# An RWKV block with a ternary feed-forward half: five tiles of lag, six-bank rounds and another order in the first tile

## The reference, cut to what matters

```python
xn = layernorm(x)                                   # eps 1e-5
# attention half (RWKV v4), input xn
h  = LN(xn) ; h1 = shift(h)                         # eps 1e-3, shift by one position
k, v, r = mix_k(h,h1) @ tm_Wk, mix_v(h,h1) @ tm_Wv, mix_r(h,h1) @ tm_Wr   # 1024x1024 each
wkv = running exponential-decay average of v weighted by exp(k)           # along the sequence
y  = xn + sigmoid(r) * wkv @ Wo
h  = LN(y) ; h1 = shift(h)
a  = y + sigmoid(mix(h,h1) @ cm_Wr) * (square(relu(mix(h,h1) @ cm_Wk)) @ cm_Wv)  # 1024->4096->1024
# feed-forward half, input xn as well
tern(W) = clip(round(W / mean|W|), -1, 1)           # over the whole 4096x1024 matrix
f  = gelu(xn @ tern(W1).T + b1) @ tern(W2).T + b2   # 1024->4096->1024
out = x + a + f
```

## Time and profile before

| what | us |
|---|---|
| median of 3 runs | 5135.28 |
| lowest of the runs | 5126.62 |
| profiled execution, device time | 5128.33 |
| its span on the slowest core (core 0) | 5126.5 |
| the other cores' spans | 5105.4 to 5123.9 |
| PE busy | 4776.4 (93%) |
| DVE busy | 2595.4 (51%) |
| ACT busy | 2131.2 (42%) |

### The profile page before, as it was taken

One profiled execution on the slowest core, in us unless ns is written; L12 is line 12 of the kernel. 1 busy time (PEld: TensorE's weight loads), 2 busy tenths in 40 slices (PEclk: granted clock), 3 DMA queues, 4 the chain that ended last, 5 costly groups with the idle time before them and its releaser, 6 DMA issues.

```text
span 5126.5 us, 63290 instructions; the slowest of 8 cores (5105.4 to 5126.5 us)
## 1 busy us (share of the span) xinstructions
PE 4776.4 (93%) x21484; PEld 2154.9 (42%) x21922; DVE 2595.4 (51%) x3424; ACT 2131.2 (42%) x3436; POOL 429.7 (8%) x807
## 2 busy tenths in 40 slices
PE   3577888799999999999999999999999999999999
PEld 1233333344444444444444444444444444444444
DVE  6746566666555545555554555545555554330111
ACT  2433756554544434354443435444343544342111
POOL 0000111122000000100000010000001000000111
PEclk8789999899999999999999999999999999999999
DMA  6477878899455564645556464555646455555765
GB/s 159 103 193 180 261 230 244 249 291 318 165 189 199 177 225 160 231 158 192 202 179 216 163 230 163 192 190 196 202 166 226 159 185 192 175 185 189 230 227 179
DMA packets 273339, 1021.40 MB, mean 199 GB/s; under 512 B 34432, under 2 KB 34560, under 8 KB 267008
## 3 DMA queue, kind: packets, MB, share of 16 engines
q1 hardware_dynamic: 194112, 706.83, 40.6%
q0 software_dynamic: 78768, 310.43, 20.7%
q10 hardware_dynamic: 144, 0.07, 0.0%
HBM read 916.52 MB, written 127.93 MB: 204 GB/s over the span
## 4 chain that ended last, share of the span: by engine, by line
PE 84%; DMA 7%; DVE 4%; issue 2%; ACT 2%; POOL 0%; another core or an unknown queue 0%; DVEq 0%; SPq 0%; ACTq 0%; POOLq 0%
PE pb L333 82%; DMA rb<-w2t 2%; DMA rb<-w1t 1%; DMA ra<-zwkvr 1%; PE pb L382 1%; PE pb L775 1%; DMA rb<-cwk 1%; DMA zw2t<-XC 1%; PE pb L779 1%; DVE xr L419 1%; DVE TT L414 0%; DMA x<-xS 0%; DVE xk L419 0%; DMA rb<-cwv 0%; ACT TT L376 0%
## 5 line engine op out<-in xcount | busy, mean ns | idle before, releaser
L333 PE MATMUL pb<-xk,rb 128*128 128x512 bf16 x8028 | 1785.6, 381 | 81.5 <-DVE xr L419 60.0
L333 PE MATMUL pb<-big,rb 128*128 128x512 bf16 x8034 | 1792.3, 379 | 16.9 <-DMA rb<-cwv 5.7
L333 PEld LDWEIGHTS pb<-xk,rb 128*128 128x128 bf16 x8192 | 802.7, 98 | 1051.9 <-issue 96.5
L333 PEld LDWEIGHTS pb<-big,rb 128*128 128x128 bf16 x8192 | 801.9, 98 | 979.2 <-issue 16.4
L796 ACT ACTIVATE RC<-pb 128x512 f32<-128x512 f32 x512 | 301.4, 589 | 725.5 <-PE pb L333 640.3
L703 ACT ACTIVATE big<-pb,vecs_s 128x512 bf16<-128x512 f32 x512 | 346.3, 686 | 563.9 <-PE pb L333 550.3
L735 DVE SCALAR_TENSOR_TENSOR RO<-pb,vecs_s,RO 128x512 f32<-128x512 f32 x128 | 95.9, 749 | 580.3 <-PE pb L333 386.2
L333 PE MATMUL pb<-xk,ra 128*128 128x512 bf16 x1005 | 255.6, 396 | 109.9 <-DMA ra<-zwkvr 44.8
L525 DVE TENSOR_TENSOR_SCAN W<-wdec,carry,pb 128x512 f32<-128x512 f32 x128 | 163.7, 1279 | 361.4 <-PE pb L333 361.4
L798 ACT ACTIVATE big<-RC 128x512 bf16<-128x512 f32 x512 | 322.5, 630 | 47.5 <-ACT RC L796 0.8
L838 DVE TENSOR_TENSOR RO<-pb,RC 128x512 f32<-128x512 f32 x113 | 77.9, 690 | 478.1 <-PE pb L333 478.1
(11 more groups left out here) (102 smaller groups left out, 3875.6 us busy)
## 6 DMA issues: line engine op xcount, KB each, us to landing
rb<-zw1t SPq DMA_DIRECT2D x256, 512.0 KB, 3.7
rb<-zw2t SPq DMA_DIRECT2D x256, 512.0 KB, 5.0
rb<-zcwk SPq DMA_DIRECT2D x240, 512.0 KB, 4.9
rb<-zcwv SPq DMA_DIRECT2D x240, 512.0 KB, 6.0
ra<-zwkvr SPq DMA_DIRECT2D x120, 768.0 KB, 7.2
resS<-RO POOLq DMA_DIRECT2D x128, 256.0 KB, 5.7
rb<-w1t POOLq DMA_DIRECT2D x64, 512.0 KB, 8.9
rb<-w2t POOLq DMA_DIRECT2D x64, 512.0 KB, 10.1
```

The source lines that it names most:

```text
L333: tok = PE(lambda t, k=k: t.matmul(pb[bank][:], slot[:, col + k * 128:col + (k + 1) * 128], rhs[k], start=start and k == 0, stop=stop and ...
```

## The change

Six things are changed together.

- `LAG` is 5: one more tile runs without a feed-forward half, and one more feed-forward half stands alone at the end. The ternary passes take a step each 5.2 us and then each 6.2 us of planned time in place of 4.2 and 5.2.
- `rounds` is new: it runs several blocks in several banks side by side, part of the reduction first. In the `LAG` tiles, six of the eight Wo blocks run over `att` pieces 0 to 6 in banks 2 to 7 as soon as piece 6 is there, and then over piece 7; six key blocks (`cwk_first`) run over each pair of `xk2` pieces as the mix delivers it. Three weight rows are released together at the end of such a round. The mixer of the next tile is held from the fourth Wo block on.
- In those tiles the k/v/r groups stand closer: first, every = (16, 4) for t = 0, (12, 4) for the middle ones, (12, 6) for the last, where they were (16, 5), (11, 5), (11, 7).
- The k/v/r rows 0 and 1 of tile 1 are fetched right after tile 0's groups; row g + 2 is fetched after group g, in place of row g + 1 before it.
- Weight loads of the start wait until all of the first `x` has landed; `R01` is made before `R0`, and `ln0_norm` waits for `R0` by its own name.
- `ln0_stats(1)` no longer stands before `wo_stage(0)`: it is chained in front of `ln0_mix(1)`, behind `ln2_apply(0)`.

The diff, cut at unchanged lines:

```diff
@@ -1,3 +1,4 @@
+import itertools
 import numpy as np
@@ -25,12 +26,12 @@
...
-LAG = 4
+LAG = 5
 NB_RING = 7
...
 BLOCK_NS = 1740.0
-SUM_NS = 4200.0
-WRITE_NS = 5200.0
+SUM_NS = 5200.0
+WRITE_NS = 6200.0
 LATE = 5
@@ -284,7 +285,7 @@
...
         rows = slice(row * 128, (row + 1) * 128)
-        ready = dma("gpsimd", f"G{ring.name}{i}", slot[:], wdram[w][rows, :], *ring.free[i])
+        ready = dma("gpsimd", f"G{ring.name}{i}", slot[:], wdram[w][rows, :], *ring.free[i], *x_in[0])
         back = dma("sync", f"W{ring.name}{i}", zdram[w][rows, :], slot[:], ready)
@@ -334,6 +335,21 @@
...
         return tok
+    def rounds(jobs, parts):
+        done = {}
+        for at, (ks, ready) in enumerate(parts):
+            for bank, slot, col, rhs, loaded in jobs:
+                for k in ks:
+                    w = [ready] if k == ks[0] else []
+                    if at == 0 and k == ks[0]:
+                        w += [loaded, *bank_free[bank]]
+                    tok = PE(lambda t, bank=bank, slot=slot, col=col, rhs=rhs, k=k: t.matmul(
+                        pb[bank][:], slot[:, col + k * 128:col + (k + 1) * 128], rhs[k], start=k == 0, stop=k == 7),
+                        w, inc=k == 7)
+                done[bank] = tok
+        return done
@@ -383,13 +399,12 @@
...
         tk["sq_free"] = t6
-        a1 = ACT(lambda s_: s_.activation(out=R0[:], in_=pb[bk2][:], func=AF.Ln, scale=1.0 / E, bias=LN0_EPS),
-                 t6, tk.get("ln0_done"), tk.get("norm_done"))
-        a2 = ACT(lambda s_: s_.activation(out=R01[:], in_=pb[bk2][:], func=AF.Ln, scale=(1.0 + LN_EPS) / E,
-                                          bias=LN0_EPS * LN_EPS))
-        bank_free[bk2] = [a2]
-        ACT(lambda s_: s_.activation(out=R0[:], in_=R0[:], func=AF.Exp, scale=-0.5), a1)
-        tk[f"rstd{j}"] = ACT(lambda s_: s_.activation(out=R01[:], in_=R01[:], func=AF.Exp, scale=-0.5), a2)
+        for r, key, scale, eps in ((R01, "rstd", (1.0 + LN_EPS) / E, LN0_EPS * LN_EPS), (R0, "rstd0", 1.0 / E, LN0_EPS)):
+            a1 = ACT(lambda s_, r=r, scale=scale, eps=eps: s_.activation(
+                out=r[:], in_=pb[bk2][:], func=AF.Ln, scale=scale, bias=eps),
+                t6, tk.get("ln0_done"), tk.get("norm_done"))
+            tk[f"{key}{j}"] = ACT(lambda s_, r=r: s_.activation(out=r[:], in_=r[:], func=AF.Exp, scale=-0.5), a1)
+        bank_free[bk2] = [a1]
@@ -460,9 +475,11 @@
...
         cur = xn[j % 2]
+        while f"rstd0{j}" not in tk:
+            yield -2000.0
         for p in range(4):
             tn = DVE(lambda v, p=p: v.tensor_mul(pair(cur, p), pair(x, p), twice(R0)),
-                     tk[f"rstd{j}"], tk.get(f"x2_free{j % 2}"))
+                     tk[f"rstd0{j}"], tk.get(f"x2_free{j % 2}"))
             yield 1220.0
@@ -505,6 +522,7 @@
...
                     yield cost
+                tk[f"mix2_{pend[3]}"] = tk["mixed"]
             elif p == 0:
@@ -564,7 +582,7 @@
...
         def last():
-            wk["nd_free"] = tk["att"] = DVE(lambda v: v.tensor_mul(ck(att, g), ND[:, 0, :], ND[:, 1, :]), l2,
+            wk["nd_free"] = tk[f"att{g}"] = DVE(lambda v: v.tensor_mul(ck(att, g), ND[:, 0, :], ND[:, 1, :]), l2,
                                             tk.get("wo_done"))
@@ -577,8 +595,6 @@
...
         unit = fetch("wkvr", g)
-        if t == 1 and g + 1 < EC:
-            prefetch("wkvr", g + 1)
         toks = []
@@ -588,6 +604,8 @@
...
         release(unit, toks[-1])
+        if t == 1 and g + 2 < EC:
+            prefetch("wkvr", g + 2)
         tk["kvr_done"] = toks[-1]
@@ -743,16 +761,25 @@
...
-    def wo_stage(t):
+    def wo_stage(t, split=False):
         short["banks"], short["at"] = [2, 3, 4, 5, 6, 7], 0
         cur = xn[t % 2]
-        unit = None
-        ev = None
+        rhs = [ck(att, k) for k in range(8)]
+        units, early = {}, {}
+        if split:
+            for r in range(3):
+                units[r] = fetch("wo", r)
+            early = rounds([(2 + c, units[c // 2][0], (c % 2) * 1024, rhs, units[c // 2][1]) for c in range(6)],
+                           [(range(7), tk["att6"]), ((7,), tk["att7"])])
         for c in range(EC):
-            if c % 2 == 0:
-                unit = fetch("wo", c // 2)
+            if c % 2 == 0 and c // 2 not in units:
+                units[c // 2] = fetch("wo", c // 2)
+            unit = units[c // 2]
             bk = short_bank()
-            tok = block(bk, unit[0], (c % 2) * 1024, [ck(att, k) for k in range(8)], True, True, unit[1], tk["att"])
+            if c in (0, 1, 2, 3, 4, 5) and split:
+                tok = early[bk]
+            else:
+                tok = block(bk, unit[0], (c % 2) * 1024, rhs, True, True, unit[1], tk["att7"])
             if c % 2:
@@ -762,6 +789,8 @@
...
                     ev, tk.get("w1_done"), tk.get("cwk_done"))
+            if split and c == 3:
+                mixer["hold"] = True
             ln.advance(BLOCK_NS, 750.0)
@@ -787,11 +816,24 @@
...
+    def cwk_first():
+        units = [fetch("cwk", r) for r in range(3)]
+        done = rounds([(2 + m, units[m // 2][0], (m % 2) * 1024, [ck(xk2, k) for k in range(8)], units[m // 2][1])
+                       for m in range(6)], [((2 * p, 2 * p + 1), tk[f"mix2_{p}"]) for p in range(4)])
+        for m in range(6):
+            if m % 2:
+                release(units[m // 2], done[2 + m])
+            cwk_evict(m, 2 + m, done[2 + m])
     def cwk_block(m, unit):
...
             release(unit, tok)
+        cwk_evict(m, bk, tok)
+    def cwk_evict(m, bk, tok):
         i = m % 2
@@ -858,7 +900,7 @@
...
-    def channel_stage(t, chunks, first, every, hooks):
+    def channel_stage(t, chunks, first, every, hooks, split=False):
@@ -871,7 +913,10 @@
...
             n += 1
-        for m in range(FC):
+        if split:
+            cwk_first()
+            n = 6
+        for m in range(n, FC):
             between()
@@ -902,20 +947,21 @@
...
             load_x(1)
-        if g == 4:
-            lane_s = ln.start(3, ln0_stats(1))
     refill(rC)
+    prefetch("wkvr", 0)
+    prefetch("wkvr", 1)
...
         ln.drain(wkv_lanes[-1])
-        ln.drain(lane_s)
+        if t:
+            ln.drain(lane_s)
         mix_lanes[:] = [ln.start(2, ln0_mix(t + 1))] if t else []
...
             plan["B"] = [("cwv", r) for r in range(2 * (EC - LATE), 16)]
-        ev, s = wo_stage(t)
+        ev, s = wo_stage(t, True)
         lane2 = ln2_stats(t, ev, s)
@@ -923,13 +969,11 @@
...
         if t == 0:
-            mix_lanes[:] = [ln.start(2, ln0_mix(t + 1))]
+            mix_lanes[:] = [ln.start(2, itertools.chain(ln0_stats(1), ln0_mix(1)))]
         lane_n = ln.start(2, ln0_norm(t + 1))
-        first, every = (16, 5) if t == 0 else (11, 5) if t < LAG - 1 else (11, 7)
-        def mixed(t=t, lane=mix_lanes[0]):
-            if t == 0:
-                prefetch("wkvr", 0)
+        first, every = (16, 4) if t == 0 else (12, 4) if t < LAG - 1 else (12, 6)
+        def mixed(lane=mix_lanes[0]):
             ln.drain(lane)
@@ -940,7 +984,7 @@
...
         hooks = {first: mixed, first + 4: normed, first + 16: stats}
-        gates = channel_stage(t, range(EC if t == LAG - 1 else EC - LATE), first, every, hooks)
+        gates = channel_stage(t, range(EC if t == LAG - 1 else EC - LATE), first, every, hooks, True)
     finish_lanes()
```

## The result

The change makes the kernel a little faster: 5082.05 to 5083.26 us, against 5120.8 to 5135.3 us before. The ratio is **0.992, 95% interval 0.9906 to 0.9934**: some 41 us. The prediction was 5034 us, 94 us less. Less than half of that came.

A forecast was written before the change was run, and what follows sets the result against it. PE, busy 4776 of 5126 us, was taken as the bound, so only its 369 us of losses before 1230 us could go. -13 - 18 - 30 - 22 - 14 - 23 + 26 = -94 from 5128.3 gave 5034 us, range 4985 to 5090.

The forecast's parts named there:

- parts 1 to 3: From the start to Wo(1): the start -13, Wo(0) with tile 1's first LN -18, the rest of tile 0 -30 us.
- last lag tile: Part 5: slower write pace shortens waits at the k group, later waits and value rows; -23 us (bounds -8 and -36).
- added tile: Part 6: a fifth lag tile loses time that a tile with its feed-forward half does not; +26 us (+12 to +50).
- The start: Part 1: x wholly landed at 11 us, with weight loads behind it, first k group at 55; -13 us.
- Wo(0) and the first LN of tile 1: Part 2: Wo(0) at 134 us, tile 1's stats moved behind it, its k group at 238; -18 us (-5 to -23).
- The rest of tile 0: Part 3: first k group of tile 1 to Wo(1) takes 122 us; -30 us (bounds -15 and -38).
- The rounds' order: Matmuls going round six banks: cost taken as 0, at most 19 us of low PE clock after waits.
- Part 4: Tiles 1 and 2: closer groups remove both `att` waits, plus smaller gains; -22 and -14 us (together -21 to -60).
- The key rounds: Tiles 1 and 2: rounds of key blocks hide the 8 us waits for the second LN's mix.
- the lag costs what it costs today: Rival: DVE's two mixes set each lag tile, rounds and closer groups only move PE's waits; -47, 5081 us, chance 0.25.
- DVE becomes the bound: Rival: clips ahead of scans and mixes in DVE's list make PE wait; up to 5162 us, chance 0.06.
- Rounds run at 1.2 GHz: Rival: all 90 matmuls of the rounds run slow, 95 us more; 5129 us, no change, chance 0.04.

The follow-up runs named there:

- e1: The changed kernel with the six-bank Wo rounds in tile 0 alone; slowest core 5071.06 us, median core 5038.6 against 5073.6 for the changed kernel.
- e8: The kernel before with one edit, the weight loads of the start wait for the first x; 5114.24 to 5129.33 us, ratio 0.9942.
- e11: e1 with `ln0_stats(1)` back in front of Wo(0); 5049.94 us, median core 5034.4.
- e4: e1 with the rounds of key blocks in tile 0 alone too; 5060.12 to 5086.61 us, ratio 0.9906.
- e12: e1 without the ternary passes' sums, mean, scaling and clips, zeros written as weights, same loads and stores; 5005.22 and 5008.63 us.
- e10: e9 with five lag tiles and the slower paces of the change; 5038.2 to 5067.25 us.
- e9: e1 with LAG 4, the old paces, and tile 1's first LN sums begun before the rounds of Wo(0); 5033.41 and 5037.55 us, ratio 0.9841.
- e3: The changed kernel with k/v/r groups every 5 blocks (7 in the last of these tiles), first at 16 and 12; 5122.72 us.

## Why the prediction was right or wrong

The sum was worked out on before's slowest core, and the slowest cores of two executions differ by more than some of its terms. So here is each part on both bases, in us saved (-) or lost (+), with e1 beside it; "median" takes the medians over the cores of the profiled executions.

| part | forecast | slowest core | median core | e1, median |
|---|---|---|---|---|
| up to Wo(1) (parts 1 to 3) | -61 | -55.4 | -61.6 | -57.5 |
| tile 1 | -22 | -9.2 | -9.5 | -18.7 |
| tile 2 | -14 | -9.8 | -7.8 | -16.8 |
| last lag tile | -23 | -17.1 | -7.5 | -16.0 |
| added tile | +26 | +44.9 | +42.1 | +33.1 |

**The start: right.** x has wholly landed at 12.2 us where 11 was forecast. 13 us were forecast in all; the first k group comes 12.5 us earlier in the median core (68.8 to 56.3), 11.5 of them by x's earlier landing (e8, 57.3), the last one by what else changed there, `R01` among it.

**Wo(0) and the first LN of tile 1: right.** Forecast were Wo(0) at 134 and the k group at 238 us, waiting for its mix and not for `zwkvr`; it was 138.46 and 244.32 in the slowest core, waiting 28.6 us for `xr`, and 137.5 and 238.5 in the median core. Wo(0) is late by 4 us, since PE waited 4.4 us for piece 6 of `att`, which DVE delivered at 138.4 and not at 134.1. e11 adds what the text did not: the earlier Wo(0) is worth 4 us at Wo(1), not 24, and e11 ends no later than e1.

**The rest of tile 0: right.** 122 us forecast, 365.92 - 244.32 = 121.6 measured. The row-2 wait is gone, the gate rows wait 4.6 us. That this stretch hits by less than 1 us is partly luck: its 16 us of waits and slow clock were set by judgement.

**The step that failed: the price of the Wo rounds.** "The rounds' order" takes 0 for it and bounds it by PE's clock alone, 0 to 19 us. Part 4 says that both `att` waits go by the closer groups, which they did, and gives the Wo round in these tiles no term at all. But if closer groups bring `att` before Wo begins, the round has nothing left to cover (2.5 us ahead of Wo(1)), and its price stands alone. That price was on another engine: DVE idles 7.7 us and then has six additions at once, 9 us in each of the tiles 1 to 4, 35 between median cores (e1). The bounds held for what they looked at and left out who else waits for the first bank. It is the larger part of what is missing in tiles 1 and 2 (-22 and -14 forecast, -9 and -10 measured; -19 and -17 in e1).

**The key rounds: right in sign.** The prediction had them hide waits of 8 us a tile. They are worth 13 us net over four tiles (e4), since the burst of evictions takes back 4 to 7 us a tile on ACT.

**The last lag tile: 17 us for 23 in the slowest core, 7.5 in the median.** The clips' idle time halved, as the step wanted (group by line in the kernel after: busy us, mean ns, idle before and its releasers; before in the earlier trace rows):

```profile
L680 DVE TENSOR_SCALAR XC<-rb 128x1024 bf16<-128x1024 int8 x64 | 43.9, 685 | 38.3 <-ACT rb L690 16.0 <-DMA zw1t<-XC 9.2 <-DMA zw2t<-XC 5.9
```

Less than half of the 39.6 us saved there reached PE. 8.5 us of the shortfall are the Wo round's; with it out the median core gains 16, 7 less than forecast, and why is open.

**The added tile: 45 us for 26 (42 in the median core).** It bore a Wo round (9 us), and the write phase now reaches into it, 16 us by e12. With the Wo round out, e10 against e9, a fifth tile costs 28 us, near the 26, though that tile itself then loses 34.1 and the last one 6 less. The slower paces were priced at 3 to 4 us in each of tiles 1 and 2; they are worth 7 and 12.

With one line changed, e1 comes near the forecast's losses in the lag tiles (29.8, 17.1, 33.1 and 29.0 us for 31, 21, 26 and 28), but part of that fit lies in the basis: the forecast started from lag tiles that lost 53.4, 35.4 and 51.2 us, where the median core lost 48.5, 33.9 and 45.0, 12.6 us less. Taken as changes, e1 still falls 18 us short of the 94: 7 in the last lag tile, 7 in the added one, 4 ahead of Wo(1), 3 in tile 1, less 3 won in tile 2. The Wo rounds are thus the largest single error, and not the whole.

**The rivals.** The time fell on the number of "the lag costs what it costs today", 5081, and its parts fit too: -61, -21 and +35 forecast, -62, -25 and +42 in the median core. It was also right that PE waits elsewhere behind the Wo rounds. Its reason, that DVE's two mixes set each lag tile, is not: e1 takes 35 us out with the same mixes, and its four lag tiles lose 109 us where before's three lose 127. "DVE becomes the bound" did not happen: DVE's busy time is what it was, it is its waiting that cost. "Rounds run at 1.2 GHz" did not happen: 47 matmuls over six banks took 10.52 us at 595.69, 224 ns each, at the clock's high level of 2.4 GHz. The rule of the Trainium skill that spoke for it ("TensorE: Matmul & The Clock Gate", section "A second HAM failure mode: psum-queue depth-cycling") does not show in these rows.

**What stays open.** With ternary work out, e12's tiles 1 to 4 still lose 70 us, and the 42 blocks behind the last lag tile lose 2 us more in the kernel after than before. Neither was taken apart. The 7 us missing in the last lag tile and the effect of closer groups on the mix (e3) are open too. Nor was the key round tried with fewer banks, which might let ACT begin its evictions sooner.

## What to carry to other kernels

Finishing several banks together hides an input that comes late, and pays only where it does come late; where the input is there in time it keeps the engine behind the matmuls idle for the length of the round and then hands it everything at once. When pricing a reordering on one engine, ask what each other engine's next instruction waits for during it. And when two parts of a change remove the same wait, count it once, and give the second its cost.

## What the runs showed of the hardware that was not expected

- A round over six banks costs PE nothing: 224 ns a matmul (10.52 us for 47). It is slow only right behind a wait, as any block is; two pieces of the first key round in tile 0 of the kernel after:

```profile
170.10 5.04 PE L348 MATMUL pb<-xk,rb 128*128 128x512 bf16 x12 [10.28 <-DVE xr L434]
176.43 2.75 PE L348 MATMUL pb<-xk,rb 128*128 128x512 bf16 x11 [1.30 <-DVE xr L434]
```

  that is 420 ns each behind 10 us of idling and 250 ns behind 1.3 us. The granted clock says the same (busy time by stretch, columns as at the top; PEclk is the third from the end): 1.00, the level of 2.4 GHz, in tile 2's Wo round, and 0.53, near that of 1.2 GHz, in the first of these pieces.

```profile
595.69:606.15 10.46, 10.41 (x49) 4.64 (x49) 2.22 (x4) 1.24 (x3) 1.60 (x3) 1.00 0.87 311
170.10:175.10 5.00, 5.00 (x12) 1.58 (x12) 4.79 (x6) 1.75 (x4) 0.00 (x0) 0.53 0.50 202
```

- One late ternary load, 12.0 us on ACT, reached PE as 7.7 us (e9), over two in-order lists, though PE had no use for that data in this stretch.
